# P.V of an attention head group placed as one block behind score bank eight, in place of two pieces

## Chip, cores and metric
The kernel runs on one core of one Trainium2 chip. The metric is device time in microseconds (us) of one execution; lower is better. The profile below comes from a separate, profiled execution.

## What is computed
The input is x with 8 batches of 512 tokens and 128 features. One post-norm transformer layer: causal attention with 16 heads of 8 dimensions, residual and layer norm, then a mixture of 14 experts with the two best per token, residual, clip and layer norm.
```
Q, K, V = x @ Wq.T + bq, x @ Wk.T + bk, x @ Wv.T + bv      # 16 heads of 8
scores  = einsum(Q, K) / sqrt(128), -inf above the diagonal
out     = einsum(softmax(scores), V) @ Wo.T + bo
x       = layernorm(x + out)
w, i    = the two best of softmax(x @ gate_w.T), w divided by its sum
moe     = sum_k w_k * (gelu(x @ w1[i_k] + b1[i_k]) @ w2[i_k] + b2[i_k])
result  = layernorm(clip(x + moe, -100, 100))
```

## The kernel before
Each engine has its own program, and they meet at semaphores. The order of the work is written out by hand: every engine walks over batches b = -1 to 8, in each over four head groups c = 0 to 3 (four heads each), and in each group over ten slots k = 0 to 9. Tables of slot numbers say what an engine does in a slot. Work for later and for earlier groups is mixed into the same slots.

TensorE does the following in a slot, in this order:
- `score_bank` (L998): one bank of 512 columns of transposed scores of this group. Ten banks make a group. There are two buffers; a bank waits for the exponentials of the bank two before (`exp_done`).
- in slot 3 (`M_AT`), `turn_maxima` (L1036) for the next group. It waits for the split maxima and for the transposition of an earlier P.V result, since both use PSUM bank `ps_o`.
- in slots 1, 3, 5, 7 and 9 (`UNIT_AT`), a `score_unit` (L975 with the mask matmuls of L983) for the group two ahead, units 0 to 4. Units only serve to find row maxima. There are two buffers; a unit waits for VectorE's reduction of the unit two before (`s_reduced`).
- `pv` (L1022) for the group before, in the slots of `PV_AT`: key tile 0 in slot 6; tiles 1, 3 and 2 in slot 9. A key tile is four matmuls, one per head, on 32 columns of the array each; in f32 every matmul stands in the trace as two. It waits for POOL's causal masks (`masked`).
- projections and their residue steps (`MISC`): q in slot 2 of group 0 with take-offs (L1050) in slots 4 and 6, va in slot 9 of group 0, vb, woa and wob (L1074, L1082) in slots 1, 3 and 5 of group 1, k in slot 2 of group 3, rk (L1088 to L1094) in slot 9 of group 3.

ScalarE takes the exponential of each bank (L806) into `probs`, which has two buffers by parity of the group, and also copies the turned maxima, parts of q and k, and values. Exponentials 0 and 2 of a group wait for P.V of the group two before (`pv_first`, `pv_filled`).

VectorE reduces every unit (L1354, `nmax`). After unit 4 it splits the maxima (L1380, L1382); at slot 0 of the next group it transposes the P.V result (L1362, `ov`), and normalises it (L1364, L1366). In group 1 it then transposes the finished rows (L1372) for the output projections woa and wob, and adds their results (L1431, L1433). Layer norm statistics and the routing (L1413 to L1494, L1615 to L1625) lie between the units. POOL masks the diagonal blocks of `probs` (L689) and sends rows to their experts. SP loads and stores.

The last two groups of batch 7 have no score units. In round b = 8 only the P.V of the last group is left of attention, in slots 6 and 9 of its group 0, between the first expert steps; then the experts follow.

The wait of a unit and that of P.V:
```
pe.wait_ge(S["s_reduced"], n - 1)
pe.wait_ge(S["masked"], 6 * n + max(PV_MASKS[j] for j in tiles))
pe.wait_ge(drained["m"], n + 3)
```
The tables of the counts that P.V waits for:
```
PV_MASKS = {0: 4, 1: 4, 3: 5, 2: 6}
PV_EXPS = {0: 7, 1: 9, 3: 9, 2: 10}
```

Of the kernel before, what the change touches and what calls it, by code (L numbers as in the profile page):

```python
# [14 lines left out]
def post_ln_attention_moe(nc, x, xT, WqT, bq, WkT, bk, WvT, bv, WoT, bo, gateT, w1, b1T, w2, b2, out):  # L15
# [47 lines left out]
    with ExitStack() as ctx:  # L63
# [193 lines left out]
                      [(0, 1, 0), (1, 1, 2 * P)])  # L257

        M_AT = 3
        PV_AT = {6: (0,), 9: (1, 3, 2)}  # L260
        PV_MASKS = {0: 4, 1: 4, 3: 5, 2: 6}
        PV_EXPS = {0: 7, 1: 9, 3: 9, 2: 10}

# [37 lines left out]
        def live(b):  # L301

            return 0 <= b < B
# [648 lines left out]
        def _(pe):  # L952
            def score_unit(b, c, u):

                n = (b * NG + c) * NUNIT + u
                if c == 0 and b == 0:
                    if u < 2:

                        pe.wait_ge(S["stacked_act"], 1 + 2 * u)
                        pe.wait_ge(S["stacked_dve"], 2 + u)  # L960
                elif u == 0:

                    pe.wait_ge(qk_loaded[c], 48 * (b + 1 if c else b))
                if n == 1:

                    pe.wait_ge(S["gate_centred"], 1)
                if not (n < 2):
                    pe.wait_ge(S["s_reduced"], n - 1)


                for h in range(2):
                    bank = ps_s[:, (c + u) % 2, h, :]
                    for e, i, at in UNIT_PARTS[u]:
                        w = P * (i + 1)
                        pe.matmul(bank[:, at:at + w], qst[:, c, e, P * i:P * i + P], kst[:, c, h, e, 0:w],  # L975
                                  start=(at == 0), stop=False, skip_group_check=True)
                    if u < 2:
                        diag_blocks = bank[:, 3 * P:T].rearrange("p (n w) -> p n w", w=P)
                    elif u < 4:
                        diag_blocks = bank[:, 2 * P:T].rearrange("p (n w) -> p n w", w=P)  # L980
                    else:
                        diag_blocks = bank.rearrange("p (n w) -> p n w", w=2 * P)[:, :, P:2 * P]
                    pe.matmul(diag_blocks, bident[:], bmask[:, 0:diag_blocks.shape[1], :],  # L983
                              start=False, stop=True, skip_group_check=True).then_inc(S["s_filled"], 1)
# [21 lines left out]
            def pv(b, c, tiles):  # L1006
                n = b * NG + c
                if last_group(b, c):
                    pe.wait_ge(S["exp_done"], NBANK * n + max(PV_EXPS[j] for j in tiles))
                else:  # L1010
                    pe.wait_ge(S["masked"], 6 * n + max(PV_MASKS[j] for j in tiles))
                if 0 in tiles:
                    pe.wait_ge(drained["vb"], b + 1)

                    if live(ahead(b, c, 2)[0]):
                        pe.wait_ge(drained["m"], n + 3)
                    else:
                        pe.wait_ge(drained["ot"], n)
                for j in tiles:
                    for g in range(4):  # L1020
                        at, w = seg(g, j)
                        last = pe.matmul(ps_o[32 * g:32 * g + 32, P * j:T], vst[:, j, 4 * c + g, :],  # L1022
                                         probs[:, c % 2, g // 2, at:at + w], start=(j == 0), stop=(j == 2),
                                         skip_group_check=True)
                    if j == 0:
                        last.then_inc(S["pv_first"], 1)
                if 2 in tiles:
                    last.then_inc(S["pv_filled"], 1)
# [69 lines left out]
            def body(b, odd):  # L1098
                for c in range(NG):
# [10 lines left out]
                    for k in range(NBANK):  # L1110
# [4 lines left out]
                        if k in UNIT_AT and live(sb_):  # L1115
                            score_unit(sb_, sc_, UNIT_AT[k])
                        if k in PV_AT and live(pb_):
                            pv(pb_, pc_, PV_AT[k])
                        if (b, c) == (0, 2) and k in FOLD_AT:
# [636 lines left out]
```

## Time and profile before
| | |
|---|---|
| median of 3 runs | 498.77 us |
| lowest, highest | 498.0, 500.38 us |
| span of the profiled execution | 529.2 us |
| the profiled execution's own time | not on the page; the span stands alone |
| instructions | 11188 |
| TensorE, VectorE, ScalarE, POOL busy | 84%, 74%, 62%, 52% of the span |
| granted TensorE clock over the span | 0.949 |

The span runs from the first to the last instruction of one profiled execution. Its times are read as places and lengths within that execution; the three runs give the time of the kernel. Ends of matmuls are modelled and include the time in which the array drains, so neighbouring rows of TensorE overlap: how long something holds TensorE is the distance between the starts of neighbouring rows. Some matmul records are missing from the trace.

### The profile page before, as it was taken

The numbers are of one execution on the slowest core, as the hardware profiler recorded it, in microseconds if no ns is written. First come the engines' busy times: TensorE is split into PE (matmuls) and PEld (weight loads), VectorE is DVE, ScalarE is ACT, GpSimd is POOL, SyncE is SP. The second block draws the span as 40 slices with busy tenths as digits, with TensorE's granted clock in tenths as the row PEclk, the third lists the DMA queues.
The fourth block names the chain that finished last, engine by engine and source line by source line (L and its number), as shares of the span: only waits on it lengthen the run. The fifth ranks groups of instructions, "written<-read, shape, count | busy, mean of one in ns | idle before, by whom it ended". The sixth has DMA issues, their size and how long they took to land.

```text
span 529.2 us, 11188 instructions
## 1 busy us (share of the span) xinstructions
PE 442.3 (84%) x3577; PEld 279.2 (53%) x3610; DVE 389.1 (74%) x979; ACT 328.7 (62%) x810; POOL 275.6 (52%) x443
## 2 busy tenths in 40 slices
PE   8799999999999999999999898685687867776980
PEld 2355454454454454454454453264586866675970
DVE  7978889988989989989989998558444544442192
ACT  5285766776777776776776667456265766565045
POOL 6033234266456456456546557826655655656363
PEclk9999999999999999999999999989578898989896
DMA  6646595552542542452542311232333322221463
GB/s 179 194 150 185 162 279 162 159 152 82 169 152 83 171 151 77 147 178 77 159 138 87 102 52 30 74 83 78 103 108 97 82 71 69 69 63 32 144 215 119
DMA packets 74393, 64.60 MB, mean 122 GB/s; under 512 B 9030, under 2 KB 68685, under 8 KB 74336
## 3 DMA queue, kind: packets, MB, share of 16 engines
q1 hardware_dynamic: 68240, 55.01, 35.3%
q0 software_dynamic: 4512, 8.54, 5.0%
q8 instruction: 30, 0.49, 0.4%
q10 hardware_dynamic: 1584, 0.34, 0.3%
q14 instruction: 27, 0.22, 0.1%
HBM read 36.88 MB, written 25.46 MB: 118 GB/s over the span
## 4 chain that ended last, share of the span: by engine, by line
PE 47%; DVE 26%; issue 8%; ACT 7%; another core or an unknown queue 5%; DMA 3%; POOL 2%; ACTq 0%; SPq 0%; DVEq 0%; POOLq 0%
DVE nmax L1354 15%; PE psum L1022 9%; PE psum L1189 8%; PE psum L998 7%; PE psum L975 6%; PE psum L1206 6%; PE psum L983 3%; DMA experts<-o_dram 2%; DVE ov L1362 2%; PE psum L1043 2%; PE psum L1050 2%; PE psum L1181 2%; ACT probs L806 2%; PE psum L1082 1%
## 5 line engine op out<-in xcount | busy, mean ns | idle before, releaser
L806 ACT ACTIVATE probs<-psum 128x512 f32<-128x512 f32 x320 | 180.2, 596 | 85.2 <-PE psum L998 45.6
L1354 DVE TENSOR_REDUCE nmax<-psum 128x2 f32<-128x1024 f32 (+3 forms) x224 | 196.3, 911 | 23.7 <-PE psum L983 23.2
L689 POOL TENSOR_SCALAR_AFFINE_SELECT probs<-probs 128x512 f32<-128x512 f32 x186 | 85.0, 484 | 125.6 <-ACT probs L806 124.9
L975 PE MATMUL psum<-kst,qst 128*128 128x512 bf16 (+2 forms) x511 | 109.6, 300 | 6.4 <-DVE nmax L1354 5.6
L757 POOL DMA_INDIRECT o_dram<-probs,xs x77 | 76.8, 997 | 59.0 <-DVE probs L1583 34.0
L998 PE MATMUL psum<-qst,kst 128*128 128x128 bf16 (+3 forms) x480 | 102.0, 296 | 6.5 <-issue 2.9
L1022 PE MATMUL psum<-probs,vst 128*32 128x512 f32 (+3 forms) x1024 | 83.1, 442 | 0.1
L983 PE MATMUL psum<-bmask,bident 128*128 128x256 bf16 (+1 forms) x320 | 80.5, 251 | 0.1
L998 PEld LDWEIGHTS psum<-qst,kst 128*128 128x128 bf16 x512 | 40.4, 98 | 54.6 <-ACT probs L806 32.1
L975 PEld LDWEIGHTS psum<-kst,qst 128*128 128x128 bf16 x512 | 47.1, 98 | 32.9 <-DVE nmax L1354 12.3
L1189 PE MATMUL psum<-xsT,kst 128*128 128x128 f32 x148 | 27.3, 314 | 17.5 <-ACT hT_sb L919 11.5
L1189 PE MATMUL psum<-xsT,w_cur 128*128 128x128 f32 x160 | 28.8, 309 | 14.5 <-ACT hT_sb L919 6.0
L1022 PEld LDWEIGHTS psum<-probs,vst 128*32 128x32 f32 x1024 | 25.5, 109 | 28.8 <-issue 24.2
L983 PEld LDWEIGHTS psum<-bmask,bident 128*128 128x128 bf16 x320 | 31.3, 98 | 12.6 <-issue 0.2
L919 ACT ACTIVATE hT_sb<-psum,w_cur 128x128 f32<-128x128 f32 x80 | 25.3, 375 | 19.2 <-PE psum L1189 12.7
L1583 DVE TENSOR_TENSOR probs<-psum,w_cur 128x128 f32<-128x128 f32 x40 | 11.4, 287 | 34.3 <-PE psum L1206 22.6
L919 ACT ACTIVATE hT_sb<-psum,kst 128x128 f32<-128x128 f32 x74 | 23.4, 374 | 19.9 <-remote 12.4
L911 ACT ACTIVATE xsT<-psum 128x128 f32<-128x128 f32 x77 | 21.9, 286 | 20.6 <-PE psum L1181 12.9
L1189 PEld LDWEIGHTS psum<-xsT,kst 128*128 128x128 f32 x148 | 22.9, 222 | 19.9 <-issue 19.9
L1189 PEld LDWEIGHTS psum<-xsT,w_cur 128*128 128x128 f32 x160 | 24.7, 221 | 16.4 <-issue 12.0
L1206 PE MATMUL psum<-w_cur,hT_sb 128*128 128x128 f32 x160 | 26.6, 292 | 3.3 <-ACT hT_sb L919 1.7
L1583 DVE TENSOR_TENSOR probs<-psum,kst 128x128 f32<-128x128 f32 x37 | 10.6, 288 | 25.3 <-PE psum L1206 14.0
(217 smaller groups left out, 709.8 us busy)
## 6 DMA issues: line engine op xcount, KB each, us to landing
kst<-dk SPq DMA_DIRECT2D x62, 128.0 KB, 3.0
qst<-dq SPq DMA_DIRECT2D x31, 256.0 KB, 3.1
xs<-xs_dram SPq DMA_DIRECT2D x77, 66.0 KB
experts<-o_dram SPq DMA_DIRECT2D x7, 512.0 KB, 4.4
dk<-k SPq DMA_DIRECT2D x7, 384.0 KB, 2.7
dq<-q SPq DMA_DIRECT2D x7, 384.0 KB
xT_sb<-in_xT SPq DMA_DIRECT2D x8, 256.0 KB
xTv_sb<-in_xT SPq DMA_DIRECT2D x8, 256.0 KB, 3.4
```

The costliest lines, as they stand in the source:

```text
L689: pool.affine_select(out=view, in_=view, compare_op=ALU.is_ge, fill=0.0, base=0, pattern=[[0, view.shape[1]], [1, P]], channel_multiplier= ...
L757: pool.indirect_dma_start(o_dram, bass.IndirectOffsetOnAxis(xs[:, u, D:D + 1].bitcast(I32), 0), y_sb[:, u, :], None, bounds_check=TOPK * N ...
L806: act.activation(probs[:, c % 2, p, kk * T:(kk + 1) * T], ps_t[:, k % 2, :], ACT.Exp, scale=SCALE).then_inc(S["exp_done"], 1)
L919: last = act.activation(hT_sb[:, j % RING, P * ch:P * ch + P], psum[:, 2 + j % 2, P * ch:P * ch + P], ACT.Gelu, bias=expert(j)[:, B1_AT + ...
L975: pe.matmul(bank[:, at:at + w], qst[:, c, e, P * i:P * i + P], kst[:, c, h, e, 0:w], start=(at == 0), stop=False, skip_group_check=True)
L983: pe.matmul(diag_blocks, bident[:], bmask[:, 0:diag_blocks.shape[1], :], start=False, stop=True, skip_group_check=True).then_inc(S["s_fill ...
L998: last = pe.matmul(ps_t[:, k % 2, at % T:at % T + w], kst[:, c, g % 2, pair, P * j:P * j + P], qst[:, c, pair, P * j:T], start=True, stop= ...
L1022: last = pe.matmul(ps_o[32 * g:32 * g + 32, P * j:T], vst[:, j, 4 * c + g, :], probs[:, c % 2, g // 2, at:at + w], start=(j == 0), stop=(j ...
L1189: last = pe.matmul(psum[:, 2 + first % 2, P * ch:P * ch + P], expert(first)[:, P * ch:P * ch + P], xsT[:, first % RING, :], start=True, st ...
L1206: last = pe.matmul(y_bank(second), hT_sb[:, second % RING, P * ch:P * ch + P], expert(second)[:, W2_AT + P * ch:W2_AT + P * ch + D], start ...
L1354: last = dve.tensor_reduce(o, i, AX.X, ALU.max, negate=True)
L1583: dve.tensor_tensor(y_sb[:, y_of % STEP, :], y_bank(y_of), expert(y_of)[:, B2_AT:WCOLS], ALU.add).then_inc(S["y_copied"], 1)
```

## The change
One line of the table changes. P.V of all four key tiles is issued in slot 8, thus behind bank 8 and ahead of bank 9 and unit 4. With all tiles in one call, the call waits for the largest of the mask counts.
```
-        PV_AT = {6: (0,), 9: (1, 3, 2)}
+        PV_AT = {8: (0, 1, 3, 2)}
         PV_MASKS = {0: 4, 1: 4, 3: 5, 2: 6}
         PV_EXPS = {0: 7, 1: 9, 3: 9, 2: 10}
```
Only TensorE's order changes. In it, the piece from slot 6 of group 3 of a batch to slot 0 of the next group. L998 is a score bank, L1050 a take-off of k, L975 with L983 a score unit, L1022 P.V. Before, slots 6 to 8 (the start of bank 8):
```order
L998 MATMUL psum<-qst,kst 128x512
L1022 MATMUL psum<-probs,vst 32x512 x4
L1050 MATMUL psum<-k,nident 128x512
L998 MATMUL psum<-qst,kst 128x384
L998 MATMUL psum<-qst,kst 128x128
L975 MATMUL psum<-kst,qst 128x384
L975 MATMUL psum<-kst,qst 128x128
L983 MATMUL psum<-bmask,bident 128x256
L975 MATMUL psum<-kst,qst 128x384
L975 MATMUL psum<-kst,qst 128x128
L983 MATMUL psum<-bmask,bident 128x256
L998 MATMUL psum<-qst,kst 128x384
```
After, the same place up to unit 3:
```order
L998 MATMUL psum<-qst,kst 128x512
L1050 MATMUL psum<-k,nident 128x512
L998 MATMUL psum<-qst,kst 128x384
L998 MATMUL psum<-qst,kst 128x128
L975 MATMUL psum<-kst,qst 128x384
```
The first P.V piece is gone from between bank 6 and the take-off. The second place is the end of the group, from the second half of bank 8 to bank 0 of the next group. Before:
```order
L998 MATMUL psum<-qst,kst 128x128
L998 MATMUL psum<-qst,kst 128x256 x2
L975 MATMUL psum<-kst,qst 128x256 x2
L983 MATMUL psum<-bmask,bident 128x2x128
L975 MATMUL psum<-kst,qst 128x256 x2
L983 MATMUL psum<-bmask,bident 128x2x128
L1022 MATMUL psum<-probs,vst 32x384 x4
L1022 MATMUL psum<-probs,vst 32x128 x4
L1022 MATMUL psum<-probs,vst 32x256 x4
L998 MATMUL psum<-qst,kst 128x512 x2
```
After:
```order
L998 MATMUL psum<-qst,kst 128x128
L1022 MATMUL psum<-probs,vst 32x512 x4
L1022 MATMUL psum<-probs,vst 32x384 x4
L1022 MATMUL psum<-probs,vst 32x128 x4
L1022 MATMUL psum<-probs,vst 32x256 x4
L998 MATMUL psum<-qst,kst 128x256 x2
L975 MATMUL psum<-kst,qst 128x256 x2
L983 MATMUL psum<-bmask,bident 128x2x128
L975 MATMUL psum<-kst,qst 128x256 x2
L983 MATMUL psum<-bmask,bident 128x2x128
L998 MATMUL psum<-qst,kst 128x512 x2
```
Sixteen P.V matmuls stand between bank 8 and bank 9, and none is left between unit 4 and the next group's bank 0. The orders of VectorE, ScalarE, POOL and SP are the same in both kernels.

## Rows read from the trace of the kernel before
**Rows 1.** The page: busy time and share; the chain by engine; one costly group
```profile
PE 442.3 (84%) x3577; PEld 279.2 (53%) x3610; DVE 389.1 (74%) x979; ACT 328.7 (62%) x810; POOL 275.6 (52%) x443
...
PE 47%; DVE 26%; issue 8%; ACT 7%; another core or an unknown queue 5%; DMA 3%; POOL 2%; ACTq 0%; SPq 0%; DVEq 0%; POOLq 0%
...
L1022 PE MATMUL psum<-probs,vst 128*32 128x512 f32 (+3 forms) x1024 | 83.1, 442 | 0.1
```
**Rows 2.** Stretches: length, busy us (instructions) of PE, PEld, DVE, ACT, POOL, clock, DMA
```profile
160.00:200.00 40.00, 38.02 (x331) 19.61 (x333) 36.36 (x83) 28.61 (x59) 22.56 (x40) 1.00 0.43 132
...
360.00:420.00 60.00, 43.52 (x282) 40.43 (x282) 32.72 (x109) 34.59 (x120) 37.24 (x38) 0.77 0.35 96
```
**Rows 3.** Waits between 60 and 320 us: us in total, times, longest
```profile
DVE nmax L1354 <- PE psum L983: 16.4, 21, 1.1
...
PEld psum L1022 <- POOL probs L689: 3.5, 11, 0.3
```
**Rows 4.** Timeline of TensorE around P.V, group 2: start, length, instructions
```profile
167.64 0.38 PE L998 MATMUL psum<-qst,kst 128*128 128x512 bf16 x1
...
167.95 1.06 PE L1022 MATMUL psum<-probs,vst 128*32 128x512 f32 x8
...
168.95 0.39 PE L998 MATMUL psum<-qst,kst 128*128 128x384 bf16 x2
...
170.82 0.27 PE L983 MATMUL psum<-bmask,bident 128*128 128x256 bf16 x1
...
171.02 1.50 PE L1022 MATMUL psum<-probs,vst 128*32 128x384 f32 x24
```
**Rows 5.** Timeline of TensorE, groups 0 and 1: units 2, 3, 4; wob; bank 6
```profile
187.22 0.38 PE L975 MATMUL psum<-kst,qst 128*128 128x384 bf16 x2
...
189.63 0.38 PE L975 MATMUL psum<-kst,qst 128*128 128x384 bf16 x2
...
190.72 0.38 PE L975 MATMUL psum<-kst,qst 128*128 128x256 bf16 x2
...
198.17 0.75 PE L1082 MATMUL psum<-wo_sb,onT_sb 128*128 128x142 f32 x4
...
198.76 0.38 PE L998 MATMUL psum<-qst,kst 128*128 128x512 bf16 x1
```
**Rows 6.** Timeline of VectorE, one batch: reductions of units, and the addition of wob
```profile
162.81 1.22 DVE L1354 TENSOR_REDUCE nmax<-psum 128x4 f32<-128x1024 f32 x1
...
167.20 1.21 DVE L1354 TENSOR_REDUCE nmax<-psum 128x2 f32<-128x1024 f32 x1
...
172.56 1.21 DVE L1354 TENSOR_REDUCE nmax<-psum 128x4 f32<-128x1024 f32 x1
...
177.59 1.22 DVE L1354 TENSOR_REDUCE nmax<-psum 128x2 f32<-128x1024 f32 x1
...
180.49 2.41 DVE L1354 TENSOR_REDUCE nmax<-psum 128x2 f32<-128x768 f32 x3
...
184.88 1.22 DVE L1354 TENSOR_REDUCE nmax<-psum 128x2 f32<-128x1024 f32 x1
...
188.08 1.29 DVE L1354 TENSOR_REDUCE nmax<-psum 128x2 f32<-128x768 f32 x2 [0.36 <-PE psum L983]
...
190.48 2.42 DVE L1354 TENSOR_REDUCE nmax<-psum 128x2 f32<-128x768 f32 x3 [1.04 <-PE psum L983]
...
197.71 0.41 DVE L1433 TENSOR_TENSOR y<-psum,xbo 128x256 f32<-128x256 f32 x1
...
203.13 1.22 DVE L1354 TENSOR_REDUCE nmax<-psum 128x4 f32<-128x1024 f32 x1
```
**Rows 7.** Timeline, the first group with P.V: unit 2; reductions of units 3 and 4
```profile
36.62 0.38 PE L975 MATMUL psum<-kst,qst 128*128 128x384 bf16 x2
...
39.67 2.42 DVE L1354 TENSOR_REDUCE nmax<-psum 128x2 f32<-128x768 f32 x3 [0.90 <-PE psum L983]
```

## The prediction
> **What bounds the kernel now.** I read the page first: busy shares and the chain that ended last [rows 1]. TensorE is busy 84% of the 529.2 us span and holds 47% of the chain, VectorE 74% and 26%; ScalarE has 7%. So two engines share the path, and the page can't say where either decides. The stretches of 40 us do [rows 2]: in the attention part TensorE is busy 38.0 us of 40 and VectorE 36.4, at a granted clock of 1.00. Neither has 10% to spare, so what matters is how they hand over to each other. The waits between 60 and 320 us [rows 3] show 21 waits of VectorE for the mask matmul of a score unit (L983), 16.4 us in all. They are the holes in VectorE's day.
>
> The handover is narrow. A score unit may start only when VectorE has reduced the unit two before it (the wait on s_reduced), so VectorE never has more than two units in hand, about 2.5 us of work at 1.2 to 1.3 us a unit [rows 6]. Everything that TensorE does between two units has to be shorter than that, or VectorE starves.
>
> **The change, in one group.** Nothing is added or removed. All P.V matmuls of a group now stand between bank 8 and bank 9, thus between unit 3 and unit 4. From the timeline of TensorE [rows 4]: bank 6 starts at 167.64 and a bank of 512 columns takes 0.21, so the first P.V piece occupies 167.85 to 168.95, 1.10 us with its entry. The second starts at 171.02, about 0.10 after the last mask matmul is through, and lasts 1.44 (its row says 1.50, of which 0.06 is drain, as 1.06 against 1.00 shows for the first). The block is 0.10 + 1.00 + 1.44 = 2.55 us; one entry of 0.1 us is saved in each of 32 groups, 3 us if TensorE alone decided.
>
> Before, unit 4 starts 190.72 - 189.63 = 1.09 us after unit 3 [rows 5]. After, 1.09 + 2.55 = 3.64 us. VectorE's reduction starts 0.86 us after its unit does (187.22 to 188.08) [rows 5, 6]. So **the reduction of unit 4 can't start before the start of unit 3 plus 4.50 us**, while in those 4.5 us VectorE has little more than unit 3 itself (1.3 us), the rest of unit 2, and small routing work.
>
> What is late next: behind unit 4's reduction stand, on VectorE's own queue, the splitting of the maxima, the transposition of the P.V result and the normalisation. TensorE's turning of the maxima in slot 3 waits for that transposition, unit 2 waits for unit 0's reduction, and in group 1 of a batch the output projections wait too. Before, the second P.V piece lay exactly there and gave TensorE 1.44 us of work while VectorE caught up; that cover is gone.
>
> **Four groups worked out.** A batch is four groups, and the trace repeats every 40.3 us (unit 4's reduction in group 1 starts at 162.81 and again at 203.13 [rows 6]). I take one batch and push each wait through with the durations of its rows. Unit 3 may start 0.04 after the end of unit 1's reduction.
> - Group 2: unit 1's reduction ends 167.20 + 1.21 = 168.41, so unit 3 starts at 168.45 and unit 4's reduction at 172.95, against 172.56 [rows 6]: +0.4. Small, because routing work (L1481, L1483) stood before it on VectorE anyway.
> - Group 3: VectorE's chain from there to the end of unit 1's reduction is unbroken (177.59 + 1.22 = 178.81) and moves by 0.4: unit 3 at 179.2, unit 4's reduction at 183.7. Before it began 1.2 us before the end of the row at 180.49, at 181.7 [rows 6]: +2.0.
> - Group 0: the chain from unit 4's reduction to the end of unit 0's reduction is 186.10 - 181.7 = 4.4 us, so it ends at 188.1. The first small products follow, then unit 1's reduction, done at 189.5. The second take-off of q waits for ScalarE and was hidden behind the first P.V piece; I put 0.4 for it (an estimate, nearly two banks of 0.21): unit 3 at 189.9. Unit 4's reduction is at 194.4, against 191.7: +2.7.
> - Group 1: VectorE's chain from unit 4's reduction to the bias addition of L1433 is 198.12 - 191.7 = 6.4 us, so it ends at 200.8. The second output projection (0.59 us), banks 6 and 7 (0.43) and unit 3 follow: unit 3 at 201.9, unit 4's reduction at 206.4, against 203.13 [rows 5, 6]: +3.3.
>
> The state at the end is the one at the start, so **each batch costs 3.3 us**. Cycles from group 2 to the next group 1 with both P.V and score units: seven, 23.1 us. The first P.V group before them, group 1 of batch 0: unit 2 starts at 36.62, banks 6 and 7 follow, unit 3 is at 37.75, unit 4's reduction at 42.25, against 39.67 + 2.42 - 1.2 = 40.9 [rows 7]: +1.4. The last two groups of the last batch have no score units; P.V there costs TensorE what it did, and the last group's P.V moves among expert steps. I take zero, with -1 and +2 as ends: up to 1 us of TensorE's lateness is absorbed since bank 0 no longer stands behind P.V, and up to two blocks' lateness (1 us each) falls on the first table and its loads.
>
> POOL's masks: the weight loads of P.V waited for them, 3.5 us in 11 waits [rows 3]. Two slots later these go. The matmul rows themselves show no such wait, so I count nothing; 3.5 us is the other end. ScalarE's exponentials need P.V of two groups before, which is issued ahead of the bank that they read: nothing. POOL, SP and the DMA queues keep their order; their work moves with the groups.
>
> **Sum**: 1.4 + 23.1 = 24.5 us. The page gives the profiled execution no time of its own beside its span of 529.2 us, 30.4 above the median of 498.77. The durations are from a stretch at full clock, so I add them unscaled: 498.8 + 24.5 = 523.3 us, 4.9% slower.
>
> The block's length, 2.55 us, is the number on which all this turns, and it is read from the places of neighbouring rows. One P.V matmul lasts 442 ns in the mean [rows 1]; 32 of them in rounds of four, end to end, would be 3.5 us. The trace shows the 32 in 2.44 [rows 4], so rounds overlap. The Trainium skill (TensorE: Matmul & The Clock Gate, Part 3) gives a packed group the length of one matmul plus about 4 ns for each further tile; by that the block would be about 3.5 us and the loss some 28 us larger (29 groups, 1 us each). The trace does not agree, and decides.
>
> **Rivals.**
> - A, TensorE decides everywhere and VectorE's holes are harmless. For it: 95% busy, 47% of the chain. Then only the saved entries count, 32 x 0.1 = 3 us, and perhaps the 3.5 us of mask waits: 492 to 496 us, faster. Decided by whether VectorE's delay at unit 4 exceeds the slack before slot 3 of the next group. Against it: VectorE is at 91%, and even behind a piece of 1.0 us it sits idle 1.04 us (the row at 190.48) [rows 6]. Chance 0.05.
> - B, the two effects cancel: the holes cost, but only in groups whose VectorE has no routing work, and the chain absorbs most of it. Inside 0.5%, 496.3 to 501.3 us. Chance 0.05.
> - C, half: TensorE has more slack before slot 3 than I count, so that a batch loses only what group 3 loses (2.0 - 0.4 = 1.6 us): 498.8 + 1.4 + 11.2 = 511 us. Chance 0.2.
> - D, routing work and projections cover nothing: each of 29 groups pays 1.6 us, 46 in all, 545 us. For it: batch 0 has no routing work. Against it: group 2, by its rows. Chance 0.05.
> - E, TensorE's new waits let the clock fall. In the stretch from 360 us it is 0.77 [rows 2], between 2.4 and 1.2 GHz; in the attention part it stays at 1.00 with TensorE 95% busy. If a tenth of the 290 us of attention ran at 1.2 GHz, its 29 us would take as long again: over 550 us with the rest. Against it: the new waits are under 1 us each. Chance 0.03. The Trainium skill (same page, Part 1) has the array at half clock after idleness; by that rule this rival would need idle stretches longer than the rows give.
>
> **How the numbers follow.** My forecast has 0.62. Its own range is 516 to 531. The batch price lies between 2.4 us (the block without its 0.1 entry, and each of four handovers 0.1 shorter) and 4.1 us (each 0.2 longer), 17 to 29 us in seven batches, beside the 1.4 and the ends of -1 and +2. With C the range reaches down to 508; 534 takes in a little more than the upper end. A, B, D and E stay out, 0.18 together. A measurement here can tell about 0.5% from no change. Faster by more 0.05, within 0.05, slower 0.90.
>
> **What would show it.** The period of the four groups goes from 40.3 to 43.6 us. VectorE's waits for L983 go from 16.4 us to over 30 us between 60 and 320, nearly all ahead of unit 4's reduction, 1 to 2 us each except in group 2. TensorE shows new waits for the transposition (L1036) and for reductions (L975), and the mask waits of P.V's weight loads are gone. The P.V block starts about 2.5 us before bank 9. The clock stays at 1.00. I am wrong if unit 4's reduction follows its predecessor without a hole, or if holes are there and the period is not longer: then TensorE had slack that I did not see.

## The result, and the profile after
The change makes the kernel slower: 534.73 us in the median of 4 runs (532.94 to 535.44) beside 498.82 (498.0 to 500.38, 4 runs), ratio 1.0707 with the interval 1.0682 to 1.0733. That is +36 us. The forecast was +24.5, 523.3 us; 534.73 lies just outside the range of 508 to 534.

One thing has to be said first, because the spans would mislead. The span after is 533.7 us and fits its runs. The span of before, 529.2 us, is 30 us above its runs: that profile was taken in a condition in which this kernel takes about 531 us (experiment e0). Comparing the two spans would give +4.5 us. The places within the attention part, though, hardly depend on the condition. The kernel after was profiled in both, and its 29th transposition of a P.V result starts at 355.47 us in the first comparison and at 355.07 in a0. Of the kernel before there are two profiles, both in the slower condition, and they agree to 0.13 us: 324.85 in the profile of before, 324.72 in e0. So all that follows compares places in the attention part.

The page after, the parts that answer to [rows 1]:
```profile
PE 439.1 (82%) x3610; PEld 274.5 (51%) x3610; DVE 395.6 (74%) x979; ACT 333.1 (62%) x810; POOL 278.6 (52%) x443
...
PE 42%; DVE 28%; DMA 8%; issue 7%; ACT 6%; POOL 4%; SPq 3%; ACTq 1%; DVEq 0%; POOLq 0%
...
L1354 DVE TENSOR_REDUCE nmax<-psum 128x2 f32<-128x1024 f32 (+3 forms) x224 | 197.3, 912 | 50.7 <-PE psum L983 50.4
L1022 PE MATMUL psum<-probs,vst 128*32 128x512 f32 (+3 forms) x1024 | 78.6, 449 | 0.0
```
Busy times have hardly moved. What moved is the idle time ahead of VectorE's reductions: 50.7 us over the whole span, nearly all of it for the mask matmul that ends a unit (L983); in before it was 23.7. The same stretch and the same waits as [rows 2] and [rows 3]:
```profile
160.00:200.00 40.00, 35.32 (x315) 18.73 (x313) 32.91 (x77) 25.61 (x52) 20.06 (x36) 1.00 0.42 123
```
```profile
DVE nmax L1354 <- PE psum L983: 36.9, 26, 2.2
...
PE psum L1036 <- DVE ov L1362: 7.2, 11, 1.0
...
PE psum L975 <- DVE nmax L1354: 5.2, 10, 0.5
...
PE psum L1050 <- ACT q L818: 4.8, 12, 0.5
```
TensorE went from 38.0 to 35.3 us busy in 40, VectorE from 36.4 to 32.9: both lose, at a clock of 1.00. The wait of VectorE grew from 16.4 us [rows 3] to 36.9, in 26 holes, one about each group. The waits of P.V's weight loads for POOL's masks are gone.

TensorE in slots 7 to 9 of group 3 and the first slots after it (start, length, instructions, idle before):
```profile
192.78 0.39 PE L975 MATMUL psum<-kst,qst 128*128 128x384 bf16 x2 [0.51 <-DVE nmax L1354]
...
193.75 2.36 PE L1022 MATMUL psum<-probs,vst 128*32 128x512 f32 x32
196.05 0.39 PE L998 MATMUL psum<-qst,kst 128*128 128x256 bf16 x2
196.28 0.38 PE L975 MATMUL psum<-kst,qst 128*128 128x256 bf16 x2
...
199.23 1.13 PE L1043 MATMUL psum<-xT_sb,wq_sb 128*128 128x512 f32 x2 [0.56 <-DVE nxt L1442]
...
201.84 0.39 PE L1050 MATMUL psum<-q,nident 128*128 128x512 bf16 x1 [0.45 <-ACT q L818]
```
Unit 3 starts at 192.78 and unit 4 at 196.28, 3.50 us later. VectorE in the same batch, the reductions of unit 4 and the transpositions:
```profile
176.10 1.23 DVE L1354 TENSOR_REDUCE nmax<-psum 128x4 f32<-128x1024 f32 x1 [1.43 <-PE psum L983]
...
177.93 0.71 DVE L1362 STREAM_TRANSPOSE ov<-psum 128x512 f32<-128x512 f32 x1
...
186.13 1.23 DVE L1354 TENSOR_REDUCE nmax<-psum 128x4 f32<-128x1024 f32 x1 [0.82 <-PE psum L983]
...
188.00 0.71 DVE L1362 STREAM_TRANSPOSE ov<-psum 128x512 f32<-128x512 f32 x1
...
197.13 1.23 DVE L1354 TENSOR_REDUCE nmax<-psum 128x4 f32<-128x1024 f32 x1 [1.44 <-PE psum L983]
...
199.01 0.17 DVE L1442 TENSOR_TENSOR nxt<-nxt,psum 128x14 f32<-128x14 f32 x1
199.09 0.71 DVE L1362 STREAM_TRANSPOSE ov<-psum 128x512 f32<-128x512 f32 x1
...
208.51 1.23 DVE L1354 TENSOR_REDUCE nmax<-psum 128x4 f32<-128x1024 f32 x1 [2.20 <-PE psum L983]
...
210.14 0.71 DVE L1362 STREAM_TRANSPOSE ov<-psum 128x512 f32<-128x512 f32 x1
...
222.20 0.71 DVE L1362 STREAM_TRANSPOSE ov<-psum 128x512 f32<-128x512 f32 x1
```
Here are the holes of 0.8 to 2.2 us ahead of every unit 4. The transposition marks each group once, and so serves as a clock for where the time went:

| from transposition to transposition | before | after | more | forecast |
|---|---|---|---|---|
| start to the first | 42.49 | 44.00 | 1.5 | 1.4 |
| first to second (group 2 of batch 0) | 10.36 | 13.18 | 2.8 | 0.4 |
| group 2 (from 164.43 / 177.93) | 9.75 | 10.07 | 0.32 | 0.4 |
| group 3 | 9.46 | 11.09 | 1.63 | 1.6 |
| group 0 | 9.67 | 11.05 | 1.38 | 0.7 |
| group 1 | 11.44 | 12.06 | 0.62 | 0.6 |
| second to 29th (27 groups) | 272.00 | 298.29 | 26.3 | 22.7 |
| behind the 29th, to the median | 174.0 | 179.3 | 5.3 | 0 |

The four group rows are one batch, 3.95 us more; the last column takes the 23.1 us of the prediction less the 0.4 of its second row. In sum 1.5 + 2.8 + 26.3 + 5.3 = 35.9 us. For before the last row uses attention places from the one condition and a median from the other; it needs that attention takes the same in both. The two profiles of the kernel after show that to 0.4 us; for before it is taken over from there. The 27 groups are not seven batches of 3.95 us: the first three of them cost 1.6 us together, the five full batches behind them 19.2 together, and the last batch 5.5.

### The profile page after: what moved, and what is told of

It reads as the page before. It is cut to its first block, busy times and chain, and to the rows that moved or that the text cites. A ratio compares the mean times of both kernels' runs of the same rounds, so it can differ in the third digit from the quotient of the medians.

```text
span 533.7 us, 11221 instructions
## 1 busy us (share of the span) xinstructions
PE 439.1 (82%) x3610; PEld 274.5 (51%) x3610; DVE 395.6 (74%) x979; ACT 333.1 (62%) x810; POOL 278.6 (52%) x443
## 4 chain that ended last, share of the span: by engine, by line
PE 42%; DVE 28%; DMA 8%; issue 7%; ACT 6%; POOL 4%; SPq 3%; ACTq 1%; DVEq 0%; POOLq 0%
DVE nmax L1354 15%; PE psum L1022 14%; PE psum L975 7%; PE psum L998 6%; POOL o_dram L757 4%; DVE ov L1362 3%; DMA o_dram<-probs,xs 3%; PE psum L983 3%; DMA experts<-o_dram 2%; PE psum L1206 2%; PE psum L1043 2%; DMA xs<-xs_dram 2%; PE psum L1189 2%; ACT q L818 2%; PE psum L1050 1%
## 5 line engine op out<-in xcount | busy, mean ns | idle before, releaser
L1354 DVE TENSOR_REDUCE nmax<-psum 128x2 f32<-128x1024 f32 (+3 forms) x224 | 197.3, 912 | 50.7 <-PE psum L983 50.4
L689 POOL TENSOR_SCALAR_AFFINE_SELECT probs<-probs 128x512 f32<-128x512 f32 x186 | 86.7, 485 | 157.3 <-ACT probs L806 156.7
L975 PE MATMUL psum<-kst,qst 128*128 128x384 bf16 (+3 forms) x512 | 110.6, 301 | 11.7 <-DVE nmax L1354 10.4
L998 PE MATMUL psum<-qst,kst 128*128 128x512 bf16 (+3 forms) x512 | 111.6, 302 | 4.3 <-ACT probs L806 2.2
L983 PE MATMUL psum<-bmask,bident 128*128 128x256 bf16 (+1 forms) x320 | 80.7, 252 | 0.0
L1022 PE MATMUL psum<-probs,vst 128*32 128x512 f32 (+3 forms) x1024 | 78.6, 449 | 0.0
L998 PEld LDWEIGHTS psum<-qst,kst 128*128 128x128 bf16 x512 | 42.3, 98 | 48.7 <-ACT probs L806 20.6
L975 PEld LDWEIGHTS psum<-kst,qst 128*128 128x128 bf16 x512 | 46.2, 98 | 40.3 <-DVE nmax L1354 23.4
L1022 PEld LDWEIGHTS psum<-probs,vst 128*32 128x32 f32 x1024 | 29.4, 112 | 40.5 <-issue 40.4
L983 PEld LDWEIGHTS psum<-bmask,bident 128*128 128x128 bf16 x320 | 31.3, 98 | 12.2 <-issue 0.5
L911 ACT ACTIVATE xsT<-psum 128x128 f32<-128x128 f32 x77 | 21.1, 275 | 18.3 <-PE psum L1181 18.1
L1181 PE MATMUL psum<-ident,xs 128*128 128x128 f32 x77 | 23.1, 300 | 11.2 <-DMA xs<-xs_dram 10.3
L945 ACT ACTIVATE xr<-xr,fin_off,fin_rs 128x128 f32<-128x128 f32 x32 | 12.6, 480 | 30.9 <-POOL fin_off L785 30.9
L1189 PE MATMUL psum<-xsT,w_cur 128*128 128x128 f32 x160 | 25.1, 281 | 1.4 <-ACT xsT L911 1.4
L1593 DVE COPY w_cur<-experts 128x642 f32 x40 | 21.1, 534 | 6.7 <-DVE probs L1583 2.3
L931 ACT ACTIVATE probs<-ident,gw 128x128 f32<-128x128 f32 x64 | 25.5, 399 | 0.0
L919 ACT ACTIVATE hT_sb<-psum,kst 128x128 f32<-128x128 f32 x74 | 23.1, 364 | 3.4 <-PE psum L1189 3.3
L1362 DVE STREAM_TRANSPOSE ov<-psum 128x512 f32<-128x512 f32 x32 | 22.7, 709 | 2.4 <-PE psum L1022 2.4
```

The costliest lines, as they stand in the source:

```text
L689: pool.affine_select(out=view, in_=view, compare_op=ALU.is_ge, fill=0.0, base=0, pattern=[[0, view.shape[1]], [1, P]], channel_multiplier= ...
L919: last = act.activation(hT_sb[:, j % RING, P * ch:P * ch + P], psum[:, 2 + j % 2, P * ch:P * ch + P], ACT.Gelu, bias=expert(j)[:, B1_AT + ...
L998: last = pe.matmul(ps_t[:, k % 2, at % T:at % T + w], kst[:, c, g % 2, pair, P * j:P * j + P], qst[:, c, pair, P * j:T], start=True, stop= ...
L1189: last = pe.matmul(psum[:, 2 + first % 2, P * ch:P * ch + P], expert(first)[:, P * ch:P * ch + P], xsT[:, first % RING, :], start=True, st ...
L1354: last = dve.tensor_reduce(o, i, AX.X, ALU.max, negate=True)
L1362: dve.transpose(ov[:].rearrange("p n w -> p (n w)"), ps_o).then_inc(drained["ot"], 1)
```

## The experiments
All ran in the condition of about 531 us, each beside runs of before on the same chip. "Late" is how much later than in e0 the 29th transposition starts. The period of a batch is the mean of five, from the 6th transposition to the 26th.

| kernel | P.V (slot: key tiles), other edit | median, us | before beside it | ratio, interval | late, us | period, us | TensorE waits: VectorE / ScalarE, us |
|---|---|---|---|---|---|---|---|
| e0 | as before | 531.51 | 531.22 | | 0 | 40.5 | 6.2 / 4.1 |
| a0 | as after | 562.02 | 529.51 | 1.0543 to 1.0659 | 30.4 | 44.3 | 21.1 / 5.7 |
| e2 | 6: 0; 8: 1 3 2 | 563.34 | 531.22 | 1.0579 to 1.0645 | 30.5 | 44.5 | 21.8 / 2.6 |
| e3 | 8: 0; 9: 1 3 2 | 548.26 | 531.22 | 1.0241 to 1.0364 | 15.6 | 43.0 | 4.2 / 11.3 |
| e1 | 9: all | 547.84 | 531.22 | 1.0301 to 1.0363 | 13.3 | 43.0 | 1.7 / 18.3 |
| e4 | 8: all, unit 4 ahead of it | 539.59 | 529.51 | 1.0129 to 1.0242 | 5.8 | 41.4 | 3.7 / 14.8 |
| e10 | 6: 0; 8: 1 3 2, unit 4 ahead of it | 543.33 | 531.50 | 1.0155 to 1.0272 | 8.5 | 41.7 | 1.8 / 19.0 |
| e9 | as before, unit 4 in slot 8 | 533.33 | 531.50 | 1.0012 to 1.0058 | 0.8 | 40.8 | 5.0 / 5.2 |
| e8 | 6: 0; 8: 1; 9: 3 2 | 540.63 | 531.50 | 1.0128 to 1.0238 | 7.8 | 41.6 | 7.7 / 4.9 |
| e6 | as after, rk in slot 8 | 558.58 | 529.51 | 1.0489 to 1.0619 | 26.8 | 43.5 | 19.2 / 4.1 |
| e5 | as after, last three groups as before | 559.85 | 529.51 | 1.0483 to 1.0613 | 31.4 | | 21.5 / 5.7 |
| e7 | as after, first two groups as before | 561.36 | 531.50 | 1.0514 to 1.0617 | 28.4 | | 22.3 / 5.3 |

The last column sums the waits of TensorE's matmuls between 60 and 320 us by the engine that ended them. It is less than what is lost, since a wait can also stand at a weight load, but its two numbers tell the kinds of loss apart: VectorE in a0, e2 and e6, ScalarE in e1, e3, e4 and e10. In all but e5 the median is 1 to 4 us further above before than the attention part is late; that rest lies behind the 29th transposition and is not explained.

### The condition: e0 and a0
e0 is the kernel before, unchanged.
```diff
 no edit
```


> The kernel before, unchanged, for a second profile. The profiled execution shown of it spans 529.2 us beside timed runs of 498.8, and its stretch from 372 to 400 us has a clock of 0.62. If that extra lies in the expert part, this execution has the same attention part (the transposition L1362 of group 2 of batch 7 near 324.9 us, a batch every 40.3 us) and a shorter rest, a span near 498 us. If it lies in the attention part, the batch period is below 40.3 us here, and my prices were read from stretched rows.

The span was 529.8 us and the run 531.51, and the runs beside it had a median of 531.22. The expected 498 did not come. Attention was in place (transposition at 324.72), so the extra 30 us stand behind it. a0 is the kernel after, unchanged.
```diff
 no edit
```


> The changed kernel, unchanged. The kernel before took 498.8 us in its first runs and 531.2 beside e0 to e3, so absolute times of different calls can't be set side by side. Here both run together. If the change costs the same in every condition, the difference is near 36 us; if the expert part's extra time of the slower condition takes in or adds to it, the difference is another, but the transposition of group 2 of batch 7 is at 355.5 us again, 30.6 later than before.

+32.5 us, and the attention part is late by 355.07 - 324.72 = 30.4, as in the first comparison (30.6). Behind it only 2.1 us are left, in place of 5.3. So 30 us of the loss come again, and the rest differs between the two conditions.

### Which of the two pieces: e2, e3, e1
e2 brings the first piece back to slot 6 and leaves the second ahead of unit 4:
```diff
-        PV_AT = {8: (0, 1, 3, 2)}
+        PV_AT = {6: (0,), 8: (1, 3, 2)}
```


> Tile 0 stays in slot 6; tiles 1, 3, 2 go to slot 8, behind bank 8 and ahead of bank 9. Theory: 1.5 us stand between units 3 and 4 in place of 2.5, and the cover behind unit 4 is lost all the same: about half of the loss, 508 to 524 us, with holes of 0.3 to 1 us ahead of unit 4's reduction. Rival (block size alone): 1.5 us is within the 2.5 us that VectorE has in hand, so 497 to 502 us.

All of the loss is there, not half. Between 60 and 320 us:
```profile
DVE nmax L1354 <- PE psum L983: 32.9, 38, 1.3
...
PE psum L1036 <- DVE ov L1362: 7.5, 6, 1.3
```
VectorE starves almost as much, in 38 shorter holes in place of 26: a piece now stands ahead of unit 3 and another ahead of unit 4. A shorter block helps nothing if the second piece still lies on the wrong side of unit 4. What e2 does not separate is the lost cover behind unit 4 from the sum of both pieces between units 2 and 4, which is nearly that of the kernel after.

e3 leaves the second piece in slot 9 and moves only the first, from slot 6 to slot 8 (diff to the kernel after):
```diff
-        PV_AT = {8: (0, 1, 3, 2)}
+        PV_AT = {8: (0,), 9: (1, 3, 2)}
```


> Tile 0 goes to slot 8, the rest stays in slot 9. Theory: 1.1 us between units 3 and 4, the cover of 1.44 us behind unit 4 kept: 497 to 506 us. If the first piece's absence from slot 6 costs by itself (take-offs of q and k no longer hidden): 506 to 515 us.

It costs 15.6 us of attention and 17.0 us in the median. My theory had at most 7 us over before; the rival had 7 to 16, so the rival is right and a little low. VectorE waits for L983 for 17.7 us, little more than in before. ScalarE lost its cover. The take-offs of q and k wait for parts that ScalarE copies; the first two lines are those waits between 60 and 320 us, in before they are 2.7 and 1.4 us:
```profile
PE psum L1050 <- ACT q L818: 5.1, 12, 0.5
...
PE psum L1050 <- ACT k L818: 4.1, 9, 0.7
```
```profile
221.42 0.39 PE L998 MATMUL psum<-qst,kst 128*128 128x384 bf16 x2 [2.11 <-ACT probs L806]
```
The timeline row shows the largest hole, 2.11 us of TensorE ahead of one score bank for an exponential. As I read these waits, the piece in slot 6 gave TensorE 1.1 us of work just where ScalarE had copies and exponentials to do.

e1 puts all four tiles behind unit 4, in slot 9:
```diff
-        PV_AT = {8: (0, 1, 3, 2)}
+        PV_AT = {9: (0, 1, 3, 2)}
```


> P.V as one block in slot 9, behind unit 4. Theory (what counts is TensorE's work between units 3 and 4, and the cover behind unit 4): VectorE has units 3 and 4 in hand when the block starts, and the block covers their reduction. It waits about 0.9 us for the end of P.V before the transposition, but TensorE is still the later one. 495 to 503 us. Rival (a block of 2.5 us starves VectorE wherever it stands): 525 to 537 us.

I had expected no change and got 16.6 us. The waits between 60 and 320 us:
```profile
DVE ov L1362 <- PE psum L1022: 12.2, 12, 1.8
...
DVE nmax L1354 <- PE psum L983: 8.8, 18, 0.7
...
PE psum L998 <- ACT probs L806: 5.1, 6, 0.9
PE psum L1050 <- ACT q L818: 5.1, 12, 0.5
```
VectorE's units come sooner than in before. By the waits, the loss is in ScalarE's cover and in the transposition, which now has to wait for the end of a block that it would have met half done; the shares of the two were not separated.

### Unit 4 ahead of the block: e4, e10, e9
If VectorE's hole ahead of unit 4 is the cause, unit 4 ahead of the block must take most of the loss away. e4 is the kernel after with
```diff
-        UNIT_AT = {1: 0, 3: 1, 5: 2, 7: 3, 9: 4}
+        UNIT_AT = {1: 0, 3: 1, 5: 2, 7: 3, 8: 4}
```


> The changed kernel with unit 4 moved from slot 9 to slot 8, where TensorE issues it ahead of the P.V block; bank 9 stays behind the block. VectorE's reduction of unit 4 and the split move with it. Theory (VectorE is starved by P.V ahead of unit 4, and gets no cover behind it): nearly all of that goes, and what is left is what e1 lost, about 13 us of attention time, the batch near 43 us. Rival (bank 9 behind the block starves ScalarE, and that is the loss): the batch stays at 44.2 us.

It does: 22.4 us of the 32.5 are gone (562.02 to 539.59). The waits between 60 and 320 us:
```profile
DVE nmax L1354 <- PE psum L983: 11.7, 27, 0.7
...
PE psum L998 <- ACT probs L806: 7.3, 19, 0.5
...
PE psum L1050 <- ACT q L818: 5.1, 12, 0.5
```
VectorE's waits fall from 36.9 to 11.7 us and TensorE no longer waits for the transposition (L1036). What is left shows as waits for ScalarE again, as in e3 and e1. It is less than I expected: 5.8 us of attention and a batch of 41.4 us, where I had 13 and 43. So what e1 loses is not simply carried over.

e10 does both: the first piece in slot 6 for ScalarE, unit 4 ahead of the second piece for VectorE.
```diff
-        PV_AT = {8: (0, 1, 3, 2)}
+        PV_AT = {6: (0,), 8: (1, 3, 2)}
-        UNIT_AT = {1: 0, 3: 1, 5: 2, 7: 3, 9: 4}
+        UNIT_AT = {1: 0, 3: 1, 5: 2, 7: 3, 8: 4}
```


> Unit 4 in slot 8, tile 0 in slot 6, tiles 1, 3, 2 in slot 8 behind unit 4 and ahead of bank 9: e2 with unit 4 ahead of the piece. Theory (VectorE's side is settled by the order of unit 4 and the piece, and the piece in slot 6 covers ScalarE): both covers are there, e2's 30 us are gone, within 3 us of before. Rival (bank 9 behind 1.5 us of P.V starves ScalarE): 5 to 10 us slower than before, as e4.

Of e2's 30.5 us 22 are gone, by that one edit, but 8.5 stay, so the rival holds (the median is 11.8 us above before, somewhat more than its 5 to 10). TensorE waits for ScalarE's exponentials, and in this place the wait comes one bank behind the piece:
```profile
PE psum L998 <- ACT probs L806: 15.8, 24, 1.4
```
```profile
185.90 1.50 PE L1022 MATMUL psum<-probs,vst 128*32 128x384 f32 x24
187.34 0.39 PE L998 MATMUL psum<-qst,kst 128*128 128x256 bf16 x2
188.42 0.39 PE L998 MATMUL psum<-qst,kst 128*128 128x512 bf16 x1 [0.43 <-ACT probs L806]
```
Bank 9 comes only behind the piece, so ScalarE is out of work meanwhile (it waits 1.62 us, until 187.77), and TensorE then waits for it. Why e10 is slower than e4, which has its whole block at that place, stays open. One difference between 60 and 320 us is that e10's weight loads of P.V wait 7.0 us for POOL's masks, 22 times, and e4's 0.2; no run tests what that is worth.

e9 is the kernel before, P.V in its old slots, with one edit:
```diff
-        UNIT_AT = {1: 0, 3: 1, 5: 2, 7: 3, 9: 4}
+        UNIT_AT = {1: 0, 3: 1, 5: 2, 7: 3, 8: 4}
```


> The kernel before with unit 4 (and its reduction and split) in slot 8: VectorE gets it one bank earlier, bank 9 comes after it. If the loop through VectorE still binds before, 1 to 5 us faster than before. If TensorE's own work and ScalarE's copies bind there, within 2 us, and slower by up to 3 if the later bank 9 delays ScalarE.

+1.8 us with the interval 1.0012 to 1.0058 from ten runs: a little slower, and surely not faster. So e4's gain is no merit of unit 4 in slot 8 by itself; it is worth something only where a block would stand ahead of it.

### Half of the second piece: e8
```diff
-        PV_AT = {8: (0, 1, 3, 2)}
+        PV_AT = {6: (0,), 8: (1,), 9: (3, 2)}
```


> Of the second piece of the kernel before, tile 1 alone (about 0.7 of 1.44 us) goes from slot 9 to slot 8; tile 0 stays in slot 6, tiles 3 and 2 in slot 9. Theory (each us of P.V moved from behind unit 4 to ahead of it is lost to the loop through VectorE): about half of e2's loss, a batch of 41.8 to 42.6 us, attention 12 to 17 us longer than before. Rival (a loss sets in only once the work between units exceeds what VectorE has in hand): a batch under 41 us, 0 to 4 us in all.

7.8 us late, between the two expectations: the half piece costs a quarter of what the whole costs in e2. VectorE's waits between 60 and 320 us:
```profile
DVE nmax L1354 <- PE psum L983: 19.0, 27, 1.1
```
The loss doesn't grow in proportion to what stands ahead of unit 4. As I read it, the half that is left behind unit 4 still covers part of VectorE's chain. The waits of P.V's weight loads for POOL's masks also grew, from 3.8 us in e0 to 7.8, and the share of that was not tested.

### The group that I had under-priced: e6
The residue step rk in slot 9 of group 3 and the projection of q in slot 2 of group 0 use the same PSUM bank. The projection waits until VectorE has read rk (L1442), which is the row at 199.01 and the 0.56 us at 199.23 above. e6 is the kernel after with rk one slot earlier, ahead of the block:
```diff
-            (3, 2): "k", (3, 9): "rk"}
+            (3, 2): "k", (3, 8): "rk"}
...
-        SHARED_AT = {(1, 4): "woa", (1, 6): "wob", (3, 9): "rk"}
+        SHARED_AT = {(1, 4): "woa", (1, 6): "wob", (3, 8): "rk"}
...
-            n = ORDER.index((3, 9) if misc_of(b)[c, k] == "rk" else (c, k))
+            n = ORDER.index((3, 8) if misc_of(b)[c, k] == "rk" else (c, k))
```


> The changed kernel with the rank matmuls rk, and VectorE's reading of them, in slot 8 of group 3 in place of slot 9. Then VectorE reads them in its hole ahead of unit 4 and the q projection of group 0 finds its bank free. Theory (the wait of the q projection for L1442, 0.56 us a batch, is what my working of group 0 left out): that wait is gone, VectorE's chain behind unit 4 is 0.33 us shorter, the batch is 0.5 to 0.8 us shorter, 4 to 6 us in all. Rival (group 0 is held by the take-offs that wait for ScalarE): within 1 us of the changed kernel.

-3.4 us in the time and -3.6 in attention. The transpositions that end group 3 and group 0:
```profile
197.40 0.71 DVE L1362 STREAM_TRANSPOSE ov<-psum 128x512 f32<-128x512 f32 x1
...
207.72 0.71 DVE L1362 STREAM_TRANSPOSE ov<-psum 128x512 f32<-128x512 f32 x1
```
Their distance is 10.32 us, where after has 11.05 (199.09 to 210.14); the other three groups are as in after. The wait of L1043 is gone. The whole is below the 4 to 6 us expected, since only five batches have that wait. One more thing changed with it: VectorE's two products of L1615 between the reductions of units 0 and 1 take 0.51 and 0.43 us in after, next to masks of POOL (L689, 201.28 to 202.27), and 0.20 and 0.21 in e6, as in before (0.21 each). What of the 0.73 us is due to that was not separated.

Group 0 of the last batch has no wait of L1043, and yet it costs 3.03 us (8.40 in before, 11.43 in after and in e6). The second L1615 takes 1.31 us there, where before has 0.43, next to an addition of POOL that starts with it; the reduction of unit 1 follows it, and TensorE waits for that reduction ahead of unit 3. Rows of VectorE, POOL and TensorE in the kernel after:
```profile
334.91 1.31 DVE L1615 TENSOR_TENSOR tm<-hot_second,rank 128x56 f32<-128x56 f32 x1
...
334.89 1.26 POOL L718 TENSOR_TENSOR xbo<-xb,bo_bc 128x512 f32<-128x512 f32 x1
...
337.42 0.39 PE L975 MATMUL psum<-kst,qst 128*128 128x384 bf16 x2 [1.45 <-DVE nmax L1354]
```
In before POOL's addition runs from 308.16, behind both L1615. That the two engines hinder each other is read from these rows; no run tests it.

### The two ends: e7 and e5
In group 2 of batch 0 the kernel after loses 2.8 us where 0.4 were forecast. TensorE there, and two stretches:
```profile
47.36 0.62 PE L1161 MATMUL psum<-wv_sb,turned_w 128*128 128x14 f32 x4 [1.75 <-DVE turned_w L1329]
```
```profile
46.00:48.90 2.90, 1.54 (x13) 1.21 (x14) 2.60 (x6) 0.66 (x2) 0.00 (x0) 1.00 0.88 264
48.90:52.30 3.40, 3.40 (x20) 2.08 (x21) 2.00 (x3) 1.91 (x4) 0.41 (x1) 0.53 0.47 124
```
TensorE waits 1.75 us for VectorE (the fold of the gate's weights), and a little later the granted clock is 0.53, nearly all of it at the lower level of 1.2 GHz, for 3.4 us. Ahead of that wait lies another of 0.74 us, which ended at 44.85. e7 is the kernel after with the first two P.V groups in their old slots:
```diff
+        pv_at = {6: (0,), 9: (1, 3, 2)} if pb_ * NG + pc_ < 2 else PV_AT
```


> The changed kernel, but P.V of the first two groups in slots 6 and 9 as before. In the changed kernel the second of these groups (with the folding of the weights) took 2.8 us longer between transpositions: TensorE idle 1.75 us ahead of L1161, and behind it 3.4 us at a granted clock of 0.53. Theory (the block brings TensorE's wait over the limit and the clock falls once): the clock stays at 1.00 there, and the transposition of group 2 of batch 7 is 3.5 to 4.5 us earlier than the 355.1 us of the changed kernel. Rival (the later groups catch up on any early lateness): within 1 us of 355.1.

The wait is 0.83 us and the clock stays:
```profile
48.00:52.00 4.00, 3.84 (x45) 2.32 (x45) 2.97 (x8) 1.95 (x4) 1.36 (x3) 1.00 0.26 70
```
The fourth transposition starts at 73.80 against 77.38, 3.6 us sooner, and the 27th still 3.5 us sooner. Then, in batch 7, the clock fell after a wait of 1.45 us; in a0 the same wait (1.44 us) had passed without a fall. 1.9 us are left at the 29th, so this fall cost 1.6 us. That the early loss is wait and clock together is supported. Its two parts were not separated; if the early fall cost as much as the one of batch 7, 1.6 of the 2.8 us are the clock (an estimate). The median of e7 is 29.9 us above before beside it, where a0's is 32.5.

e5 is the kernel after with the last three P.V groups in their old slots:
```diff
+        pv_at = {6: (0,), 9: (1, 3, 2)} if pb_ * NG + pc_ >= B * NG - 3 else PV_AT
```


> The changed kernel, but P.V of the last three groups in slots 6 and 9 as before. Attention up to group 1 of batch 7 stays as in the changed kernel. Theory (about 5 us of the 36 are lost in the last groups and the first expert steps): 3 to 6 us less than the changed kernel. Rival (that rest belongs to the chip's condition, not to the placement): within 1 us of the changed kernel.

-2.2 us, with intervals that overlap those of a0: inconclusive. Its attention part had a fall of the clock of its own (lines are one further in this kernel):
```profile
336.39 0.41 PE L975 MATMUL psum<-kst,qst 128*128 128x384 bf16 x2 [1.44 <-DVE nmax L1355]
```
```profile
336.00:340.00 4.00, 3.61 (x20) 1.44 (x24) 3.03 (x8) 0.60 (x1) 1.00 (x2) 0.58 0.26 70
```
Up to there e5 had been 0.6 us ahead of a0, and at the 29th transposition it is 1.0 behind: this fall too cost 1.6 us. What the end of P.V costs among the expert steps is not settled.

## Why the prediction was right in its direction and short in size
The mechanism was right: VectorE starves ahead of unit 4 and has no cover behind it. What failed were three terms of the sum, in order of size: the end of attention and the expert steps, put at 0 (5.3 us); group 0 of a batch, put at 0.7 us (1.38, and 3.03 in the last batch); and the second P.V group, put at 0.4 us (2.8).

- **What bounds the kernel.** Right. Neither engine decides alone; the handover of unit 4 does. e4 shows it: the same block, with unit 4 ahead of it, costs a third. The rule that went with it, work between two units must be shorter than the 2.5 us that VectorE has in hand, is no safe bound: e2 has 1.5 us of P.V between units 3 and 4, and VectorE waits 32.9 us.
- **The block.** A little too long in the forecast: 2.55 us with its entry, measured 2.40 (0.10 and the 2.30 from 193.75 to 196.05). Unit 3 to unit 4 is 3.50 us against 3.64, and unit 3 to the reduction of unit 4 is 4.35 (192.78 to 197.13) against 4.50. The Trainium skill (TensorE: Matmul & The Clock Gate, Part 3) gives the length of one group of packed tiles; eight groups laid end to end at the 442 ns of [rows 1] would make the block 3.5 us, an estimate, and the measured 2.30 shows that they overlap.
- **What is late next.** Right as a list (maxima, transposition, normalisation, projections), and e2 makes it stronger: what counts is not the block ahead of unit 4 as much as the cover that is gone behind it. e2 with 1.5 us ahead of unit 4 loses as much as after with 2.3, though it also keeps 1.0 us ahead of unit 3.
- **Groups 2, 3 and 1 of a batch.** Right: 0.32, 1.63 and 0.62 against 0.4, 1.6 and 0.6.
- **Group 0: a step that failed.** I wrote that "The first small products follow, then unit 1's reduction" and added 0.4 us for the take-off of q, which does wait 0.40 (to 203.72). The projection of q itself waits 0.56 us for VectorE's reading of rk, in the shared bank. That reading comes behind unit 4's late reduction, and the projection (0.96 us on TensorE, 199.23 to 200.19) holds up the bank behind it; ScalarE's exponential of that bank and its copies of q follow, and the take-off ahead of unit 3 waits for the second copy. Group 0 costs 1.38, not 0.7. e6 takes the wait away and takes 0.73 of it back, where the forecast was 0.68 short.
- **Over the 27 groups** the forecast had 22.7 us and 26.3 were measured, 3.6 more. The seven groups 0 are 5.1 us above their forecast: five with the shared bank cost 6.7 us in place of 3.5, the first 0.3, the last 3.0. The other twenty groups are 1.5 us below. So it is luck in part that e6, five times 0.71 us, takes back just these 3.6. I also wrote that POOL's "work moves with the groups"; in the last batch it moved next to VectorE's L1615 (1.31 us in place of 0.43), and that is where this group's time shows.
- **The first groups.** +1.4 at the first transposition was right (1.5). I gave group 2 of batch 0 the price of a later group 2. It has the fold on TensorE's path, TensorE waited 1.75 us where I had argued that the new waits are under 1 us, and the clock fell. This is rival E's mechanism, once, with the wait 2.4 us above the forecast.
- **The last groups: the largest miss.** I took zero with +2 as the end. 5.3 us came, in the condition of the first comparison; 2.1 in the other. Without this term the time would have been within the range. There is no profile of before in the first condition, so where these 5.3 stand is open.
- **The rivals.** A and B are out. C (half) and D (each group the same) are out by the uneven rows of the table: 0.3 to 1.6 us. The side effect on POOL's masks was real: the 3.8 us of waits between 60 and 320 us are gone (the 3.5 in 11 of [rows 3] is what stands between 60 and 300). I argued that they are worth nothing, and no run tests that alone.
- **ScalarE at nothing.** Beyond the 0.4 us for a take-off I priced nothing here. e3 shows that taking the first piece out of slot 6 costs 15.6 us where VectorE is not held up more than before; e1 (13.3) mixes that with the late transposition. In after this price doesn't show: 15.6 us alone (e3) and 30.5 alone (e2) are 30.4 together. As I read it, while TensorE waits for VectorE, ScalarE gets its work done; the waits for ScalarE are 11.3 us in e3 and 5.7 in after.

So the misses are 3.6 us (the 27 groups), 2.4 (fold and clock) and 5.3 (the end): 11.3 of the 11.4 us between 523.3 and 534.7.

## What to carry to other kernels
Where two engines are both over 90% busy and hand buffers of depth two back and forth, price a moved block by where it stands between the producer's instructions and by the chain on the other engine that it used to cover; the busy shares tell neither, and the longest stretch alone does not either (e2 loses all with 1.5 us between units 3 and 4). Walk every wait of the walked group, shared PSUM banks too: one such bank cost 3.6 us here (e6). Losses of this kind did not add here: as I read it, while TensorE waits for one engine the other gets its work done.

## What the runs showed of the hardware that was not expected
- The same kernel takes 498.8 us in one set of runs and 531.2 in another, steadily in each; the second was seen on two chips. In the kernel after, profiled in both, the attention part is the same to 0.4 us, and 27 us lie behind it. The kernel after, from 400 to 480 us, first in the first comparison, then in a0:
```profile
400.00:480.00 80.00, 68.86 (x553) 63.95 (x551) 52.47 (x134) 66.75 (x248) 61.76 (x60) 0.97 0.41 105
```
```profile
400.00:480.00 80.00, 55.61 (x383) 51.56 (x384) 39.26 (x117) 47.60 (x172) 49.66 (x49) 0.87 0.35 94
```
In a0 all five engines do less in the same time, at a clock of 0.87. It has waits over the whole span that the first profile has not at all, with nothing in the trace that ends them:
```profile
DVE probs L1583 <- remote: 21.4, 9, 4.9
```
Their cause is open.
- The granted clock fell after waits of TensorE of 1.75 us (after), 1.44 (e5) and 1.45 (e7), each with a wait of about 0.7 us before it (0.74 ahead of 44.85 in after, 0.69 and 0.68 in e5 and e7); the stretches shown are at 0.53 and 0.58. The same pair of waits in a0 (0.69 ahead of 334.30, 1.44 ahead of 337.01) left the clock at 1.00. In e5 and e7 one such fall cost 1.6 us.
- 32 f32 matmul records of P.V on four column groups, 449 ns each in the mean, take 2.30 us in one block and 1.00 + 1.44 us in two pieces, beside some 0.1 us ahead of each block or piece.
- VectorE's L1615 took 0.20 or 0.21 us in e6 and in most batches of before, where POOL was idle for nearly all of it. It took 0.25 to 0.51 us beside POOL's L689, and 1.31 beside POOL's L718. Group 0 of the last batch, where that stands, lost 3.0 us, and the ones before it 1.4.
